# Five of ten token gathers of each expert half moved behind the second expert's GELUs, and eighteen fillers instead of eleven at the hidden biases

## What is computed

```python
x = x + 0.5 * ffn(layernorm(x), gate_w, gate_b, w1, b1, w2, b2)
x = x + attn(layernorm(x), Wq, Wk, Wv, Wa, Wg, Wo, ln1, W1, b1, W2, b2, ln2)
x = x + 0.5 * ffn(layernorm(x), gate_w, gate_b, w1, b1, w2, b2)

def ffn(tokens):                                # 8 experts, at most 160 tokens each
    probs = softmax(tokens @ gate_w + gate_b)
    expert = argmax(probs)                      # the first 160 tokens of an expert are kept
    h = gelu(dispatch(tokens) @ w1[e] + b1[e])  # 160 x 256 by 256 x 1024
    out = h @ w2[e] + b2[e]                     # 160 x 1024 by 1024 x 256
    return combine(out * prob_of_the_chosen)    # zero for a token that was dropped
```

## Time and profile before

| what | us |
|---|---|
| median of 3 executions | 702.8 (702.68 to 703.57) |
| the profiled execution | 701.53 |
| its span, first to last instruction | 699.8 |
| first expert half | 0 to about 129 |
| attention | about 129 to 593 |
| second expert half | about 593 to 700 |

### The profile page before, as it was taken

The page is one execution under the profiler, slowest core; times in us unless marked ns, Lnnn a source line. Parts: engine busy times, 40 slices in busy tenths (PEclk is TensorE's granted clock), DMA queues, the critical chain, the costliest instruction groups (busy, mean ns, idle before and its releaser), DMA issues. The chain is left out here.

```text
span 699.8 us, 12023 instructions
## 1 busy us (share of the span) xinstructions
PE 657.2 (94%) x4564; PEld 574.2 (82%) x4564; DVE 476.9 (68%) x1042; ACT 448.4 (64%) x810; POOL 193.0 (28%) x290
## 2 busy tenths in 40 slices
PE   8789999999899999999999999999998999899993
PEld 7468999576688898898898898898886788489993
DVE  6844400357979989989989989988999877510001
ACT  5224443079689899898899798897796243244440
POOL 6250111320033116216216216214233221500112
PEclk9979999999999999999999999999999999889998
DMA  8989960521011011021022022011011094207700
GB/s 271 335 280 326 357 211 23 160 86 61 31 61 50 27 46 63 15 76 56 22 76 76 1 75 76 1 46 46 1 46 46 14 375 170 65 12 248 255 23 26
DMA packets 53011, 74.10 MB, mean 106 GB/s; under 512 B 4775, under 2 KB 44796, under 8 KB 52953
## 3 DMA queue, kind: packets, MB, share of 16 engines
q1 hardware_dynamic: 48600, 59.84, 26.2%
q0 software_dynamic: 4352, 13.49, 5.4%
HBM read 58.26 MB, written 15.20 MB: 105 GB/s over the span
## 5 line engine op out<-in xcount | busy, mean ns | idle before, releaser
L1671 PE MATMUL bank<-zt_h,w_in_h 128*128 128x512 f32 x192 | 79.8, 416 | 3.5 <-DVE qg L1342 1.5
L992 PE MATMUL bank<-xdt,ring 128*128 128x160 f32 x512 | 77.2, 310 | 4.0 <-ACT hid L822 2.6
L992 PEld LDWEIGHTS bank<-xdt,ring 128*128 128x128 f32 x512 | 73.9, 198 | 6.0 <-ACT hid L822 3.3
L1671 PE MATMUL bank<-yt_h,w_h 128*128 128x256 f32 x256 | 73.6, 287 | 5.0 <-DVE yt_l L1452 2.7
L784 DVE SCALAR_TENSOR_TENSOR xo<-bank,gate,xg 128x256 f32<-128x256 f32 x20 | 9.3, 482 | 99.7 <-PE bank L1019 99.7
L1673 PE MATMUL bank<-zt_h,w_in_l 128*128 128x512 f32 x192 | 75.6, 394 | 0.0
L1672 PE MATMUL bank<-zt_l,w_in_h 128*128 128x512 f32 x192 | 75.6, 394 | 0.0
L1005 PE MATMUL bank<-hid,ring 128*128 128x160 f32 x512 | 72.8, 300 | 1.5 <-DVE idx_s L768 0.7
L1671 PE MATMUL bank<-w_h,ht_h 128*128 128x256 f32 x256 | 73.6, 288 | 0.0
L822 ACT ACTIVATE hid<-bank,b1t 128x160 f32<-128x160 f32 x128 | 50.2, 396 | 35.3 <-remote 9.7
L1005 PEld LDWEIGHTS bank<-hid,ring 128*128 128x128 f32 x512 | 70.4, 190 | 2.3 <-issue 2.3
(11 more groups left out here) (256 smaller groups left out, 1631.6 us busy)
## 6 DMA issues: line engine op xcount, KB each, us to landing
ring<-in_L_ffn_w SPq DMA_DIRECT2D x32, 1024.0 KB, 10.6
z_mid<-zb POOLq DMA_DIRECT2D x8, 512.0 KB, 3.4
zr<-z_mid SPq DMA_DIRECT2D x16, 256.0 KB, 2.8
xr<-x_mid SPq DMA_DIRECT2D x16, 256.0 KB, 3.6
out<-xq POOLq DMA_DIRECT2D x16, 256.0 KB, 4.3
zb<-x_mid SPq DMA_DIRECT2D x7, 512.0 KB, 4.5
xc<-in_L_attn_x SPq DMA_DIRECT2D x4, 512.0 KB, 4.6
ring<-in_L_attn_x SPq DMA_DIRECT2D x4, 512.0 KB, 8.1
```

Source lines behind the costliest of these rows:

```text
L992: ins = T.matmul(bank[b][:, 0:CAP], w1_of(s)[:, k, m * P:(m + 1) * P], xdt[:, k, e * CAP:(e + 1) * CAP], start=k == 0, stop=k == KD - 1)
L1671: T.matmul(out, left[0], right[0], start=start, stop=False)
```

## The change

Three things change.

1. In `expert_steps`, the five turn-ins of tiles 5 to 9 move from behind `up(1)` to behind `down(1)`, for PE and for ACT.
2. POOL waits before the gather of tile 5 until `gelu_done[3]` is 4. The gathers of tiles 5 to 9 are thus issued when the last GELU of expert 1 is done. DVE's norms of these five tiles move too: in the second half behind `idx_s`, in the first half behind piece 5 of the dense weights and ahead of piece 6.
3. At the hidden biases in attention, 18 fillers stand where 11 stood. This happens once in the program.

```diff
@@ expert_steps
                 yield "up", e
-                if e == 1:
+                yield "down", e - 1
+                if e == 2:
                     for a in TURN_IN[2]:
                         yield "turn_in", a
-                yield "down", e - 1
@@ gpsimd_program
             for a in range(ST):
+                if a == TURN_IN[2][0]:
+                    pool.wait_ge(gelu_done[3], 2 * 2)
                 nc.gpsimd.indirect_dma_start(
@@ vector_program
-            for a in range(TURN_IN[1][0], ST):
+            for a in TURN_IN[1]:
                 gather_norm(a)
@@
             if first:
                 v.wait_ge(ln1_in, 48)
+            else:
+                for a in TURN_IN[2]:
+                    gather_norm(a)
             for n, (_, hi, lo) in enumerate(pieces):
+                if n == RB + 2:
+                    for a in TURN_IN[2]:
+                        gather_norm(a)
                 v.wait_ge(raw_in[n % RB], 16 * (n // RB + 1))
@@ attention, wo
                     hidden_bias()
-                    keep_busy(11, o_attn)
+                    keep_busy(18, o_attn)
```

## The result

The changed kernel took **698.59 us** as a median of 5 executions (696.67 to 699.72), the kernel before 702.8 in the 5 executions beside it (699.05 to 704.53). The ratio is 0.9945 with a 95% interval of 0.9922 to 0.9969: faster by 4.2 us. The forecast was 697.7, a gain of 5.1. The two profiled executions stand at 701.53 and 696.67, so the traces have 4.9 us to explain.

The account below looks back on a forecast made before the run. TensorE, busy 94% of the span, was taken to bound the kernel. Gains of 4.3 (second half), 0.0 (first half) and 0.8 (fillers) made 5.1 off 701.5, so 696.4, or 697.7 as a median; range 694.8 to 702.0.

Parts of the forecast that it names:

- Second half: From `up(0)` to `up(3)`: 28.1 us instead of 32.4, so 4.3 less, 2.8 of it late signals, the rest low clock.
- the second rival: Late signals follow the gathers beside `down(0)` and `up(2)`: 1.0 lost, 1.7 more by a clock fall; 700.4, chance 0.15.
- First half: From `up(0)` on: 1.6 us gained up to `up(3)`, then 1.6 lost at half clock, so 0.0.
- The half-clock term: First half, head of `up(3)`: the clock falls after little PE work and costs 1.6 us.
- The bounds: First half's gain: from -0.8 (slower) to +2.4 (no clock fall, and DVE free 0.8 earlier).
- the forecast's own wait of 3.6 us: First half, turn-in 5: PE arrives at 65.6 and waits 3.6 us for DVE's norm, done at 69.2.
- Fillers: Hidden biases: seven more fillers prevent the clock's fall; 0.8 us gained, at most 1.1, at least 0.
- The cover of 0.7 us: Hidden biases: the added fillers end 0.7 us ahead of `yo`, so PE idles 0.7 instead of 2.2 us.
- the case that `yo` came earlier: Hidden biases: were `yo` 2.2 us earlier against PE, the seven added fillers would cost up to 1.5.
- The reading of "remote": ACT's waits at `up(0)`, 4.5 us in three: PE's signals to ACT come late while POOL issues long rows of gathers.
- the rival built on it: Second half: the new burst of turn-ins itself drops the clock and costs 1.6; 699.3, chance 0.03.
- its main term: Second half, `up(0)`: removing late signals beside gathers shortens it from 7.14 to 4.35 us, 2.8 of the 4.3 gained.

Follow-up runs that it names:

- chip 7: Set of runs with the kernel before at 699.82; the 28.51 is from the changed kernel with 11 fillers instead of 18, measured 698.63.
- chip 0: Set of runs with the changed kernel itself timed against the kernel before: 698.60 against 692.30, ratio 1.0089.
- the first chip: Where the first result was measured: changed kernel 698.59 us, kernel before 702.8, ratio 0.9945.
- chip 3: Set of runs with the kernel before at 702.49; changed kernel with ten added gathers 707.53, with first-half norms three pieces earlier 693.14.
- the moves alone: Changed kernel with 11 fillers instead of 18, against the kernel before: 698.63, ratio 0.9987.
- The trace on chip 2: Kernel before with ten plain transfers added on POOL's queue in its second half: 691.91 beside 692.05 for the kernel before (one execution each).
- the extra gathers on chip 3: Changed kernel with ten more gathers, read by nobody, behind the GELUs of expert 3 in the second half: 707.53 (one execution).

## Why the prediction was right, and where not

- **Second half, forecast 4.3, measured 3.3.** The steps held: `up(0)` 4.42 (4.35 forecast), the wait of turn-out 0 for ACT's copy 0.56 (0.45), the clock at 1.00, the first late gather 0.7 us behind `up(1)`, scatters and landing hidden. With no late signal the stretch is 28.51 (chip 7) or 28.17 (chip 0) for the 28.1 of the sum. What was missed is the second rival's delay: one signal late by 1.04 us in `up(2)`, priced at 1.0 there. It appears in the traces of the first chip and chip 3, but not in the one on chip 7. The fall of the clock that the rival added to it did not come behind `up(2)`, nor in the two traces of chip 3 with such a signal in each `up(2)`.
- **First half, forecast 0.0, measured 0.0 up to the end of `up(3)`, but by another sum.** `up(0)` began 1.1 later because the clock rose at 41.2 instead of 38.4, ahead of all that changed, and `up(2)` lost 1.0; so PE came to turn-in 5 at 67.9, not 65.6, and waited 1.3 us, not 3.6. `up(3)` began at 72.7 (72.3 forecast), since DVE's piece 5 sets it whenever PE arrives. The half-clock term of 1.6 measured 1.3. That the half came out at 0.0 was luck in part: two delays of about 1 us ahead of the wait shortened it. The bounds were too narrow on the side of the loss: -0.8 stood there, and the moves alone lost 1.8. The step that failed is the clock's price. It counted the low level only over the head of `up(3)`. So it was after the wait of 1.3 us (0.50 for 3.4 us); but behind waits of 2.4 to 4.5 us, in five traces, the low level lasted 6.8 us, and 10.2 in the one with a wait of 5.0, and the turn-ins lay in it, wholly or in part. With the forecast's own wait of 3.6 us, 1.6 was too little.
- **Fillers, forecast 0.8, measured 1.1 to 1.5.** The cover of 0.7 us was right to a tenth (0.72), and so was the mechanism. The mis-sized term is how much of the half clock reaches the path: all of the 1.1 that stood as the bound. The trace on chip 2 sharpens it. It has 11 fillers and a wait of 2.20, PE is busy 1.30 of 3.50 us from 180.4 to 183.9 as it was before the fall in the earlier trace rows (1.29), yet its clock stays at 1.00 up to 187.4, and `vn` is turned 7.92 us behind the first `wo`, as with 18 fillers (7.93). So the fillers' gain is that the fall doesn't come; and whether it comes after a wait of 2.2 us isn't fixed. Nor are the fillers free: where the clock was low while they ran, `vn` was turned 8.2 and 9.8 us behind the end of `yo`, against 8.0 in the changed kernel and 9.1 in the kernel before. The forecast had priced them only for the case that `yo` came earlier.
- **The reading of "remote"** was only argued in the forecast, which also put the first half's waits (4.5 us in three) beside the second half's `up(0)`; the second half had five, 5.2 us in all. The row of gathers is now shown as its cause by the extra gathers on chip 3 and by taking POOL's wait away or putting it in alone on chip 7. What it is in the row that delays the signal isn't shown.
- **The turn-ins don't lower the clock** where nothing but a short wait is around them: PEclk is 1.00 in 629.80 to 633.10 with PE busy 2.04 of 3.30 us. The Trainium skill, in "TensorE: Matmul & The Clock Gate", Part 4, says that transposes don't count as work for the clock in the way matmuls do; in this place the trace shows no cost of that, and the rival built on it falls. In the first half the clock fell at 71.9, during the turn-ins and behind a wait; what each of the two did to it isn't separated, but with the wait down to 0.28 us (norms three pieces earlier) it didn't fall.
- **What the forecast did not consider** is that its main term is there in some of the runs only. The traces of chips 0 and 2 have no late signals, the kernel before takes 692 us on them, and the change costs 6.3 us on chip 0, where it was timed. The forecast came true because the first result was measured where the signals are late.

## What to carry to other kernels

When an engine starts late for a signal that the profile puts down to no engine, look what POOL is issuing at that time. No signal here was late before the fourth gather of a row: keep longer rows away from stretches in which PE and ACT hand banks to each other closely, and put them where a wait is already there. If a step is moved, place the work it depends on by the time at which it is now wanted, on every engine: here the norms placed three pieces earlier were worth about 5 us more, if one compares the two ratios of 0.9871 and 0.9945, which come from different runs. The traces of chip 3 agree: from the first `up(0)` to the end of `up(3)` it takes 34.2 us, and 39.1 in the kernel with ten more gathers, whose first half is the changed kernel's. And time a change of a few tenths of a per cent on more than one chip before believing its sign.

## What the runs showed of the hardware

- The same program takes 699.8 and 702.5 us on chips 7 and 3, 702.8 in the runs of the first result, and 692.3 and 692.1 on chips 0 and 2. In the first three, signals from PE to ACT come late during long rows of gathers, most of them by 1.0 to 2.6 us. The other two show none, chip 0 not even with ten more gathers. Whether it is the chip or something else that differed between the sets of runs stays open.
- A late signal costs little by itself (1.0 us in `up(2)`). Five in a row, 8.0 us of ACT's waiting, came with 5.4 us more between `up(4)` and `up(5)` (chip 3 against chip 0), and behind them the clock was low from 658.0 to 661.5.
- Ten gathers keep POOL issuing for 12.3 us (642.14 to 654.40), ten plain transfers of the same size for 5.4.
